# Clipping the two probability pairs of an attention step in one instruction, from a joint tile with three buffers

## The chip, the cores and the metric

The kernel runs on one core of a Trainium2 chip. The metric is the device time of one execution in microseconds (us). The engines are TensorE (PE, with its weight loads shown as PEld), VectorE (DVE), ScalarE (ACT), GpSimd (POOL) and SyncE (SP, which issues DMAs).

## The reference, cut to what matters

A cross attention with 16 heads of 32 columns, then a feed-forward part. Four batch elements, 512 query rows and 1601 context rows each. What bears on the change is the attention:

```python
scores = jnp.einsum('bhsd,bhtd->bhst', q, k) / sqrt(32)
scores = jnp.clip(scores, -50.0, 50.0)
scores = jnp.where(attend, scores, -10000.0)
scores = jnp.clip(scores, -50.0, 50.0)
probs = softmax(scores); probs = probs / (probs.sum(-1) + 1e-08)
ctx = jnp.einsum('bhst,bhtd->bhsd', probs, v)
delta = layernorm(rs * (ctx @ Wo.T + bo)) * gamma + beta
x = x + delta
x = x + ffn(layernorm(x))      # Hadamard transforms, up/gate 512 -> 2048, silu, down 2048 -> 512
```

The kernel clips after the exponential instead: between exp(-50) and exp(50), the constants `LOW` and `HIGH`.

## The kernel before, in words

The function `context` handles the four batch elements one after another. For each one there is a stretch that projects the context to keys and values, and then an attention stretch. The feed-forward part (`ffn`) follows after the fourth.

An attention stretch has four chunks c of four heads. A chunk has 13 steps t, one for each tile of 128 context rows (the last has 65). `STEPS` is 52 steps for a batch element; a step is called i, and its two pairs of heads are the pairs 2i and 2i+1, called here the first and the second pair (z = 0 and z = 1). All pairs of a program are numbered N. The work of a step is:

- PE, `scores(b, i)`, L1097: 12 matmuls into two of the three PSUM buffers `sc` (each 128 x 1024). It waits once, until the first exponential of step i-1 is done, since its second pair takes the buffer of that one.
- ACT, `exps`, L864: one exponential for each pair, 128 x 1024 f32, from `sc` into the pair's `probs` buffer.
- DVE, `clips`, L995: one clip for each pair, in place.
- DVE, `add`, L958: the sum of a pair over two adjacent steps, into `padd`. Steps 2j and 2j+1 of a chunk are added to each other. The first pair's add (z = 0) is issued in the odd step 2j+1, right behind that step's clips. The second pair's add (z = 1) is issued one step later, in the even step 2j+2, again behind the clips of that step. The 13th step has no partner.
- PE, `values`, L1110: 4 products with f32 data (8 matmuls in the trace), for which both pairs of the step have to be clipped. `sums`, L1122, and `single`, L1129, add up the rows of `padd` with a matrix of ones.

PE's order is written out by hand: scores of step i+1, then `weigh` of step i-1, which is sums and values. ACT copies the products of a chunk out in step 1 of the next chunk (`collect_values`, L842) and the sums in step 4 (`collect_sums`, L848), between the two exponentials of that step. DVE also takes a small reciprocal (`chain.recips`, L278) behind the adds of step 9 of each chunk but the first.

The buffers: the first pair has three `probs` buffers, the second pair four. Before ACT writes a pair of step i it waits, on its own queue, until the step that used this buffer last is done with it: its values product, and its add (the semaphore `added[z]`). For the first pair that is step i-3, for the second pair step i-4:

```python
old = N // 2 - BUFS[n % 2]
if old >= 0:
    act.wait_ge(values_done, old + 1)
    og, ot = divmod(old, TT)
    if ot < TT - 1:
        act.wait_ge(added[n % 2], og * QP + ot // 2 + 1)
```

Of the kernel before, what the change touches and what calls it, by code (L numbers as in the profile page):

```python
# [25 lines left out]
ALU = mybir.AluOpType  # L26
ACT = mybir.ActivationFunctionType

B, S, H, T = 4, 512, 512, 1601
# [3 lines left out]
P = 128  # L33
# [6 lines left out]
LOW = float(np.float32(np.exp(-50.0)))  # L40
HIGH = float(np.float32(np.exp(50.0)))
# [576 lines left out]
def context(nc, io, scr, proj, chain, hand):  # L618
# [1 line left out]
    STEPS = HC * TT  # L620
    PAIRS_B = 2 * STEPS
    NSC = 3
    BUFS = (3, 4)
    QP = TT // 2
    SUMS = 2 * QP + 1
    SCALE = 1.0 / float(np.sqrt(HD))
# [1 line left out]
    with ExitStack() as stack:  # L628
        m = Mem(nc, stack, "cx")
# [7 lines left out]
        q = m.at("q", [P, 2, HC, S], qslab, F32R)  # L637
        slab = m.slab("slab", Room.SIZE)
        HEADS = 2 * S * 4
        probs = [[m.at(f"probs{z}_{i}", [P, 2, S], slab + (BUFS[0] * z + i) * HEADS)[:] for i in range(BUFS[z])] for z in range(2)]  # L640
        padd = [[m.at(f"padd{z}_{i}", [P, 2, S], slab + (sum(BUFS) + 2 * z + i) * HEADS)[:] for i in range(2)] for z in range(2)]
        ob, os = (m.at(n, [P, S], slab + (sum(BUFS) + 4) * HEADS + i * S * 4)[:] for i, n in enumerate(("ob", "os")))
        sc = [m.ps(f"sc{i}", [P, 2, S]) for i in range(NSC)]
        acc, tot = m.ps("acc", [P, S]), m.ps("tot", [P, S])
        kv = [sc[0][:, 0], sc[0][:, 1], sc[1][:, 0], sc[1][:, 1]]
# [9 lines left out]
        scores_done, exp_done, clip_done, values_done, sums_done = (m.sem(n) for n in (  # L655
            "scores_done", "exp_done", "clip_done", "values_done", "sums_done"))
# [13 lines left out]

        def prob(N):

            return probs[N % 2][N // 2 % BUFS[N % 2]]

        def rows_of(t):
            return TLAST if t == TT - 1 else P

        with nc.Block() as block:
# [123 lines left out]
            def _(act):  # L802
# [47 lines left out]
                def exps(b):  # L850
                    for n in range(PAIRS_B):
                        N = b * PAIRS_B + n
                        c, t = divmod(n // 2, TT)
                        r = rows_of(t)
                        act.wait_ge(scores_done, N + 1)
# [6 lines that stand above are left out]
                            else:  # L862
                                act.wait_ge(sums_done, og * SUMS + SINGLE)
                        nc.scalar.activation(prob(N)[0:r], sc[n % NSC][0:r], ACT.Exp, bias=mbias[0:r, b, t:t + 1],  # L864
                                             scale=SCALE).then_inc(exp_done, 1)
                        if c and n % 2 == 0 and t == 1:
                            collect_values(b, c - 1)
                        if c and n % 2 == 0 and t == 4:
                            collect_sums(b, c - 1)
                    collect_values(b, HC - 1)  # L870
                    collect_sums(b, HC - 1)
# [60 lines left out]
            def _(dve):  # L932
# [15 lines left out]
                def add(b, c, j, z):  # L948
                    g = b * HC + c
                    i = b * STEPS + c * TT + 2 * j  # L950
                    dve.wait_ge(clip_done, 2 * i + 3 + z)
                    if b and c == 0 and j == 0:
                        dve.wait_ge(chain.xs_stored, b * 16)
                    if g == 0 and j == 0:
                        dve.wait_ge(ugw_out, 16)
                    if j >= 2 or g:
                        dve.wait_ge(sums_done, sums_until(g, j - 2) if j >= 2 else sums_until(g - 1, QP + j - 2))
                    nc.vector.tensor_tensor(padd[z][(g * QP + j) % 2][:], prob(2 * i + z)[:], prob(2 * i + 2 + z)[:],  # L958
                                            ALU.add).then_inc(added[z], 1)
# [29 lines left out]
                def clips(b):  # L989
                    for n in range(PAIRS_B):  # L990
                        N = b * PAIRS_B + n
                        c, t = divmod(n // 2, TT)
                        r = rows_of(t)
                        dve.wait_ge(exp_done, N + 1)
                        nc.vector.tensor_scalar(prob(N)[0:r], prob(N)[0:r], LOW, HIGH, ALU.max, ALU.min).then_inc(clip_done, 1)  # L995
                        if t % 2 and n % 2:
                            add(b, c, t // 2, 0)
                        if t and t % 2 == 0 and n % 2:
                            add(b, c, t // 2 - 1, 1)
                        if c and t == 9 and n % 2:  # L1000
                            chain.recips(nc, dve, b, c - 1)
# [19 lines left out]
                for b in range(B):  # L1021
# [44 lines left out]
                    if b + 1 < B:  # L1066
                        proj.split_lo(nc, dve, b + 1, 0)
                        proj.split_lo(nc, dve, b + 1, 1)
                    clips(b)

            @block.tensor
# [431 lines left out]
def build(nc, io, out):  # L1503
    def scratch(name, shape, dt=F32):
        return nc.dram_tensor(f"scr_{name}", shape, dt).ap()

    scr = {
        "q": scratch("q", [B, P, 2, HC, S]),
        "c": scratch("c", [B, P, HC, S]),
        "sum": scratch("sum", [B, NH, S]),  # L1510
        "rec": scratch("rec", [B, NH, S]),
        "wo": scratch("wo", [P, 2, HC, H]),
        "x1": scratch("x1", [B, P, ST, H]),
        "xs": scratch("xs", [B, 2, P, HC, S]),
        "wd": scratch("wd", [P, INTER // P, 2, H]),
        "ug": scratch("ug", [P, 2, 2, HC, GC * P]),
    }

    with ExitStack() as stack:
        m = Mem(nc, stack, "all")  # L1520
        chain = Chain(m)
        proj = Projections(Mem(nc, stack, "proj"))
        hand = Handover(Mem(nc, stack, "hand"), proj.slab)
        context(nc, io, scr, proj, chain, hand)
        ffn(nc, io, scr, out, chain, hand)
# [40 lines left out]
```

## Time and profile before

| | us |
|---|---|
| median of 3 runs | 1597.52 |
| lowest, highest | 1591.58, 1601.28 |
| the profiled execution's own time | 1598.8 |
| its span | 1597.0 |
| PE busy | 1518.2 (95%) |
| DVE busy | 984.1 (62%) |
| ACT busy | 746.0 (47%) |
| mean granted TensorE clock | 0.965 |

The span runs from the first to the last instruction, so the time holds 1.8 us around it. The busy times are shares of the whole span; the attention stretches are only four parts of it, and there the shares are others.

### The profile page before, as it was taken

How to read it: one execution, taken by the hardware profiler on the slowest of the kernel's cores; microseconds unless marked ns; L12 is line 12 of the kernel's file. 1: busy time of each engine (PE TensorE's matmuls, PEld its weight loads, DVE VectorE, ACT ScalarE, POOL GpSimd, SP SyncE). 2: the span in 40 equal slices, each digit the busy share in tenths (PEclk: the TensorE clock that was granted, in tenths of full speed). 3: DMA queues.
4: the chain of work that ended last, by engine and by line, in shares of the span. 5: the costliest groups of instructions: out<-in, count | busy, mean ns of one | idle time of the engine just before them, and what ended most of it. 6: DMA issues, size and time to landing. Idle time of an engine off the chain costs nothing. (4 is left out here: it accounts for less than half of the span.)

```text
span 1597.0 us, 25675 instructions
## 1 busy us (share of the span) xinstructions
PE 1518.2 (95%) x10712; PEld 1027.0 (64%) x10712; DVE 984.1 (62%) x1548; ACT 746.0 (47%) x923; POOL 51.1 (3%) x71
## 2 busy tenths in 40 slices
PE   5999999898899989899989999899999999999998
PEld 5887333685433578433568433376888888888886
DVE  5553999585699595699685599655434333243333
ACT  4334899233699533699633699523212212112111
POOL 1000000100000100000100000000000000000000
PEclk9998999899799999799999899999999999999999
DMA  8342000643200443100442500270201001010002
GB/s 241 138 143 119 8 9 9 178 142 104 89 9 16 134 139 110 53 9 15 126 147 84 237 9 16 54 270 11 69 0 54 27 27 53 0 53 27 0 27 79
DMA packets 56252, 121.18 MB, mean 76 GB/s; under 512 B 15680, under 2 KB 35408, under 8 KB 51536
## 3 DMA queue, kind: packets, MB, share of 16 engines
q1 hardware_dynamic: 43440, 70.04, 12.9%
q0 software_dynamic: 12704, 49.61, 9.7%
q8 instruction: 80, 1.31, 0.3%
q14 instruction: 28, 0.23, 0.1%
HBM read 82.64 MB, written 36.96 MB: 75 GB/s over the span
## 5 line engine op out<-in xcount | busy, mean ns | idle before, releaser
L864 ACT ACTIVATE cx_probs<-cx_sc,proj_mbias 128x1024 f32<-128x1024 f32 (+1 forms) x416 | 442.7, 1114 | 43.0 <-PE cx_sc L1097 35.6
L995 DVE TENSOR_SCALAR cx_probs<-cx_probs 128x1024 f32<-128x1024 f32 (+1 forms) x416 | 270.1, 684 | 33.9 <-ACT cx_probs L864 32.5
L1097 PEld LDWEIGHTS cx_sc<-cx_q,cx_kt 32*128 32x128 f32 (+1 forms) x2496 | 104.4, 185 | 203.1 <-ACT cx_probs L864 185.7
L958 DVE TENSOR_TENSOR cx_padd<-cx_probs,cx_probs 128x1024 f32<-128x1024 f32 x192 | 233.8, 1218 | 1.4 <-DVE cx_probs L995 0.7
L1110 PE MATMUL cx_acc<-cx_probs,cx_vt 128*32 128x512 f32 (+1 forms) x1664 | 222.4, 607 | 3.8 <-DVE cx_probs L995 3.8
L1097 PE MATMUL cx_sc<-cx_q,cx_kt 32*128 32x512 f32 (+1 forms) x2496 | 208.0, 435 | 17.5 <-ACT cx_probs L864 14.1
L136 PE MATMUL cx_sc<-proj_cs,proj_wk 128*128 128x256 f32 (+1 forms) x1344 | 174.5, 291 | 18.0 <-DVE proj_cs L614 13.5
L136 PEld LDWEIGHTS cx_sc<-proj_cs,proj_wk 128*128 128x128 f32 x1344 | 170.1, 199 | 22.8 <-issue 16.7
L136 PE MATMUL cx_sc<-proj_wv,proj_cs 128*128 128x512 f32 (+1 forms) x624 | 164.2, 423 | 9.6 <-DVE cx_kt L939 9.6
L136 PEld LDWEIGHTS cx_sc<-proj_wv,proj_cs 128*128 128x128 f32 (+1 forms) x624 | 123.0, 200 | 42.6 <-DVE cx_kt L939 9.7
L1122 PE MATMUL cx_tot<-cx_padd,cx_ones 128*32 128x256 f32 x1536 | 120.8, 390 | 0.0
L1416 DVE SCALAR_TENSOR_TENSOR ff_hf<-ff_up,ff_scale,ff_silu 128x512 f32<-128x512 f32 x32 | 24.0, 750 | 145.8 <-ACT ff_silu L1356 145.8
L1356 ACT ACTIVATE ff_silu<-ff_gp,ff_scale 128x512 f32<-128x512 f32 x32 | 22.1, 690 | 189.6 <-PE ff_gp L136 189.6
L1416 DVE SCALAR_TENSOR_TENSOR ff_hf<-ff_up,hand_scale,ff_silu 128x512 f32<-128x512 f32 x32 | 24.0, 750 | 129.3 <-ACT ff_silu L1356 129.2
L1356 ACT ACTIVATE ff_silu<-ff_gp,hand_scale 128x512 f32<-128x512 f32 x32 | 22.1, 690 | 165.0 <-PE ff_gp L136 165.0
L136 PE MATMUL ff_yp<-hand_wds,ff_hs 128*128 128x512 f32 x384 | 96.8, 401 | 0.0
L136 PE MATMUL ff_yp<-ff_wds,ff_hs 128*128 128x512 f32 x384 | 94.7, 395 | 0.2 <-DVE ff_hs L1419 0.2
L939 DVE SCALAR_TENSOR_TENSOR cx_kt<-cx_sc,proj_bk,cx_kt 128x256 fp32r<-128x256 f32 (+1 forms) x112 | 49.2, 450 | 67.1 <-ACT cx_kt L814 66.9
L814 ACT ACTIVATE cx_kt<-cx_sc,proj_bk 128x256 fp32r<-128x256 f32 (+1 forms) x112 | 49.2, 450 | 84.1 <-PE cx_sc L136 83.9
L136 PEld LDWEIGHTS ff_yp<-hand_wds,ff_hs 128*128 128x128 f32 x384 | 73.1, 191 | 18.1 <-issue 0.5
L136 PEld LDWEIGHTS ff_yp<-ff_wds,ff_hs 128*128 128x128 f32 x384 | 72.0, 188 | 17.7 <-DVE ff_hs L1419 0.6
L1110 PEld LDWEIGHTS cx_acc<-cx_probs,cx_vt 128*32 128x32 f32 (+1 forms) x1664 | 51.5, 111 | 49.1 <-DVE cx_probs L995 10.6
(233 smaller groups left out, 1699.0 us busy)
## 6 DMA issues: line engine op xcount, KB each, us to landing
proj_raw<-in_ctxT SPq DMA_DIRECT2D x24, 512.0 KB, 4.2
scr_q<-cx_q SPq DMA_DIRECT2D x3, 2048.0 KB, 8.2
cx_wo<-scr_wo POOLq DMA_DIRECT2D x3, 2048.0 KB, 13.1
scr_xs<-cx_xs POOLq DMA_DIRECT2D x3, 2048.0 KB, 6.8
cx_q<-scr_q SPq DMA_DIRECT2D x3, 1536.0 KB, 11.0
cx_qxt<-in_x SPq DMA_DIRECT2D x4, 1024.0 KB, 9.4
scr_c<-cx_ob SPq DMA_DIRECT2D x16, 256.0 KB
cx_fl<-in_wdT POOLq DMA_DIRECT2D x4, 1024.0 KB, 7.7
```

Source lines behind the costliest of these rows:

```text
L136: last = nc.tensor.matmul(out, stationary(a, c), moving(z, c), start=first and n == 0, stop=final and n == len(parts) - 1)
L814: nc.scalar.activation(kt[:, 0, c, t0:t0 + w], kv[c][:, 0:w], ACT.Identity, bias=bk[:, c:c + 1]).then_inc(k_hi, 1)
L864: nc.scalar.activation(prob(N)[0:r], sc[n % NSC][0:r], ACT.Exp, bias=mbias[0:r, b, t:t + 1], scale=SCALE).then_inc(exp_done, 1)
L939: nc.vector.scalar_tensor_tensor(kt[:, 1, c, t0:t0 + w], kv[c][:, 0:w], bk[:, c:c + 1], kt[:, 0, c, t0:t0 + w].bitcast(F32), ALU.add, ALU. ...
L958: nc.vector.tensor_tensor(padd[z][(g * QP + j) % 2][:], prob(2 * i + z)[:], prob(2 * i + 2 + z)[:], ALU.add).then_inc(added[z], 1)
L995: nc.vector.tensor_scalar(prob(N)[0:r], prob(N)[0:r], LOW, HIGH, ALU.max, ALU.min).then_inc(clip_done, 1)
L1097: last = nc.tensor.matmul(sc[(2 * i + h // 2) % NSC][0:r, h % 2], kt[own, z, c, t * P:t * P + r], q[own, y, c], start=n == 0, stop=n == 2)
L1110: last = nc.tensor.matmul(acc[h * HD:(h + 1) * HD], vt[0:r, t, (4 * c + h) * HD:(4 * c + h + 1) * HD], prob(N + h // 2)[0:r, h % 2], start ...
L1122: last = nc.tensor.matmul(tot[h * HD:(h + 1) * HD, cols], ones[:], padd[h // 2][(g * QP + j) % 2][:, h % 2, cols], start=j == 0 and half = ...
L1356: nc.scalar.activation(silu[u % 2][:], gp[buffer(u, first)][:], ACT.Silu, scale=scale[k][:, 1, u % GC:u % GC + 1]).then_inc(silu_done, 1)
L1416: nc.vector.scalar_tensor_tensor(hf[u % 2][:], up[buffer(u, first)][:], scale[k][:, 0, u % GC:u % GC + 1], silu[u % 2][:], ALU.mult, ALU.m ...
```

## The change

The probabilities of a step's two pairs stand side by side in one tile of 128 x 4 x 512 f32. There are three of these tiles, used in turn by the steps. The second pair thus has three buffers where it had four; `padd`, `ob` and `os` keep their addresses. DVE waits in each step until both exponentials are done and clips all four heads in one instruction of 128 x 2048 elements, which counts two on `clip_done`. The ACT waits are computed by the unchanged lines quoted above from the new `BUFS`, so that for either pair the earlier user of the buffer is now step i-3. Where the adds are issued stays as it was, and so do PE's order and all amounts of work.

```diff
-    BUFS = (3, 4)
+    BUFS, PADD = (3, 3), 7
...
-        probs = [[m.at(f"probs{z}_{i}", [P, 2, S], slab + (BUFS[0] * z + i) * HEADS)[:] for i in range(BUFS[z])] for z in range(2)]
-        padd = [[m.at(f"padd{z}_{i}", [P, 2, S], slab + (sum(BUFS) + 2 * z + i) * HEADS)[:] for i in range(2)] for z in range(2)]
+        probs = [m.at(f"probs{i}", [P, 4, S], slab + 2 * i * HEADS)[:] for i in range(BUFS[0])]
+        padd = [[m.at(f"padd{z}_{i}", [P, 2, S], slab + (PADD + 2 * z + i) * HEADS)[:] for i in range(2)] for z in range(2)]
...
         def prob(N):
-            return probs[N % 2][N // 2 % BUFS[N % 2]]
+            return probs[N // 2 % BUFS[0]][:, N % 2 * 2:N % 2 * 2 + 2]
...
-                        dve.wait_ge(exp_done, N + 1)
-                        nc.vector.tensor_scalar(prob(N)[0:r], prob(N)[0:r], LOW, HIGH, ALU.max, ALU.min).then_inc(clip_done, 1)
+                        if n % 2:
+                            both = probs[N // 2 % BUFS[0]][0:r]
+                            dve.wait_ge(exp_done, N + 1)
+                            nc.vector.tensor_scalar(both, both, LOW, HIGH, ALU.max, ALU.min).then_inc(clip_done, 2)
```

## Rows read from the trace of the kernel before

**Rows 1.** Window of the first attention stretch: length, busy PE, PEld, DVE, ACT, POOL, clock, DMA

```profile
156.90:281.00 124.10, 121.49 (x1400) 46.42 (x1404) 116.59 (x152) 112.94 (x111) 1.68 (x1) 0.96 0.03 9
```

**Rows 2.** Timelines of ACT, DVE and PE in order of time, two steps of chunk 0

```profile
180.03 2.12 ACT L864 ACTIVATE cx_probs<-cx_sc,proj_mbias 128x1024 f32<-128x1024 f32 x2 [0.21 <-PE cx_sc L1097]
182.36 2.12 ACT L864 ACTIVATE cx_probs<-cx_sc,proj_mbias 128x1024 f32<-128x1024 f32 x2 [0.20 <-PE cx_sc L1097]
...
180.73 1.22 DVE L958 TENSOR_TENSOR cx_padd<-cx_probs,cx_probs 128x1024 f32<-128x1024 f32 x1
181.87 1.29 DVE L995 TENSOR_SCALAR cx_probs<-cx_probs 128x1024 f32<-128x1024 f32 x2
183.07 1.22 DVE L958 TENSOR_TENSOR cx_padd<-cx_probs,cx_probs 128x1024 f32<-128x1024 f32 x1
...
181.35 0.97 PE L1097 MATMUL cx_sc<-cx_q,cx_kt 32*128 32x512 f32 x12
```

**Rows 3.** Waits within 170 to 280 us: who waited for whom

```profile
PEld cx_sc L1097 <- ACT cx_probs L864: 38.6, 46, 0.9
ACT cx_probs L864 <- PE cx_sc L1097: 6.3, 31, 0.2
```

**Rows 4.** Groups by line and shape, DVE

```profile
L995 DVE TENSOR_SCALAR cx_probs<-cx_probs 128x1024 f32<-128x1024 f32 x384 | 249.6, 684 | 33.9 <-ACT cx_probs L864 32.5
L958 DVE TENSOR_TENSOR cx_padd<-cx_probs,cx_probs 128x1024 f32<-128x1024 f32 x192 | 233.8, 1218 | 1.4 <-DVE cx_probs L995 0.7
...
L543 DVE TENSOR_SCALAR cx_qxt<-cx_qxt,cx_mean,cx_inv 128x512 f32<-128x512 f32 x16 | 7.7, 543 | 0.1
...
L285 DVE TENSOR_TENSOR cx_ca<-cx_ca,cx_rb 128x512 f32<-128x512 f32 x12 | 7.5, 685 | 0.0
...
L278 DVE RECIPROCAL all_recip<-all_total 128x16 f32<-128x16 f32 x16 | 3.9, 246 | 39.9 <-DMA all_total<-scr_sum 39.9
```

**Rows 5.** Timeline, ACT and DVE, first step of the first stretch

```profile
156.93 2.12 ACT L864 ACTIVATE cx_probs<-cx_sc,proj_mbias 128x1024 f32<-128x1024 f32 x2
158.07 0.70 DVE L995 TENSOR_SCALAR cx_probs<-cx_probs 128x1024 f32<-128x1024 f32 x1 [1.47 <-ACT cx_probs L864]
```

**Rows 6.** Timeline, DVE, small instructions that each wait for the last

```profile
597.30 0.16 DVE L102 TENSOR_TENSOR all_tmp<-all_inv 128x4 f32<-128x4 f32 x1
597.50 0.17 DVE L104 TENSOR_TENSOR all_tmp<-all_tmp,all_ve 128x4 f32<-128x4 f32 x1
```

**Rows 7.** Timeline, DVE and ACT, an exponential that waits for an add

```profile
474.73 1.22 DVE L958 TENSOR_TENSOR cx_padd<-cx_probs,cx_probs 128x1024 f32<-128x1024 f32 x1
...
476.06 3.31 ACT L864 ACTIVATE cx_probs<-cx_sc,proj_mbias 128x1024 f32<-128x1024 f32 x3 [0.34 <-DVE cx_padd L958]
```

**Rows 8.** Timeline, ACT: chunk 0's steps 3 and 11; chunk 2 from step 0

```profile
166.09 2.12 ACT L864 ACTIVATE cx_probs<-cx_sc,proj_mbias 128x1024 f32<-128x1024 f32 x2 [1.33 <-PE cx_sc L1097]
...
184.68 2.12 ACT L864 ACTIVATE cx_probs<-cx_sc,proj_mbias 128x1024 f32<-128x1024 f32 x2 [0.20 <-PE cx_sc L1097]
...
220.09 3.31 ACT L864 ACTIVATE cx_probs<-cx_sc,proj_mbias 128x1024 f32<-128x1024 f32 x3 [0.33 <-DVE cx_padd L958]
223.31 0.60 ACT L842 ACTIVATE cx_ob<-cx_acc 128x512 f32<-128x512 f32 x1
223.81 3.35 ACT L864 ACTIVATE cx_probs<-cx_sc,proj_mbias 128x1024 f32<-128x1024 f32 x3
...
250.75 3.31 ACT L864 ACTIVATE cx_probs<-cx_sc,proj_mbias 128x1024 f32<-128x1024 f32 x3 [0.38 <-DVE cx_padd L958]
```

**Rows 9.** Windows, PE only: length, busy, granted clock, DMA share, GB/s

```profile
180.00:280.00 100.00, 100.00 (x1192) 1.00 0.03 10
560.00:573.00 13.00, 9.64 (x30) 0.74 0.46 141
```

**Rows 10.** Timeline, PE, at the lower clock, step 3 of the first stretch

```profile
164.40 1.65 PE L1097 MATMUL cx_sc<-cx_q,cx_kt 32*128 32x512 f32 x12
165.98 1.62 PE L1110 MATMUL cx_acc<-cx_probs,cx_vt 128*32 128x512 f32 x8
```

More of the change, by code:

```diff
@@ L639, in context @@
         HEADS = 2 * S * 4
-        probs = [[m.at(f"probs{z}_{i}", [P, 2, S], slab + (BUFS[0] * z + i) * HEADS)[:] for i in range(BUFS[z])] for z in range(2)]
-        padd = [[m.at(f"padd{z}_{i}", [P, 2, S], slab + (sum(BUFS) + 2 * z + i) * HEADS)[:] for i in range(2)] for z in range(2)]
-        ob, os = (m.at(n, [P, S], slab + (sum(BUFS) + 4) * HEADS + i * S * 4)[:] for i, n in enumerate(("ob", "os")))
+        probs = [m.at(f"probs{i}", [P, 4, S], slab + 2 * i * HEADS)[:] for i in range(BUFS[0])]
+        padd = [[m.at(f"padd{z}_{i}", [P, 2, S], slab + (PADD + 2 * z + i) * HEADS)[:] for i in range(2)] for z in range(2)]
+        ob, os = (m.at(n, [P, S], slab + (PADD + 4) * HEADS + i * S * 4)[:] for i, n in enumerate(("ob", "os")))
         sc = [m.ps(f"sc{i}", [P, 2, S]) for i in range(NSC)]
```

## The prediction

> **What bounds the kernel now.** The change touches only the four attention stretches, so I read these and leave the rest. First the window of one: it is 124 us long, and in it PE is busy for 121, DVE for 117 and ACT for 113 [rows 1]; the others are alike, and the four hold 495 us of the span. Three engines are nearly full, so busy time says nothing here, and I went to the timeline. There a step takes 182.36 - 180.03 = 2.33 us on ACT. ACT's two exponentials last 2.12 together, and then it waits 0.20 for the scores [rows 2]. The list of waits has the other half of that loop: PE's loads for the scores wait for ACT 46 times, ACT for the scores 31 times [rows 3]. So the period is a ring of two engines: the first exponential, the scores that need its PSUM buffer, the next first exponential. DVE is a third thing that just fits: the add starts at 180.73 and at 183.07 again, 2.34 us per step, in which the two clips hold the engine for 183.07 - 181.87 = 1.20 and the add for 181.87 - 180.73 = 1.14 [rows 2]. DVE follows behind ACT and has no slack, and at a chunk's first step an exponential already waits 0.34 us for an add [rows 7].
>
> **What the change does to DVE's work.** It removes 208 clip instructions of 684 ns and makes the other 208 twice as large. The trace has no such instruction of 2048 elements. From above: two durations, 1.37 us. From below: an instruction of the same kind with 512 elements takes 543 ns against 684 for 1024 [rows 4], though with two pointer operands; growth of 0.14 for 512 elements would give 0.97. In between: an add takes 685 ns for 512 elements and 1218 for 1024, the clip takes for 1024 what the add takes for 512 [rows 4], so it moves two elements in the time of one and should take for 2048 what an add takes for 1024: 1.22 us. I take this one, as the rate is that of its own 1024 row. Behind an instruction that it doesn't depend on, the next one starts 0.08 before the recorded end (1.22 against 1.14 for the add), so the joint clip holds DVE for 1.14 against 1.20: a gain of 0.06 us a step. The Trainium skill (VectorE: DVE Perf Modes, section on the perf-mode tier table) gives 1227 ns for an f32 tensor_scalar of 2048 elements; the rows come to the same.
>
> **What it adds: two dependences.** The joint clip can't start before the second exponential is done. A clip that finds DVE free starts 158.07 - 156.93 = 1.14 us after the start of its exponential [rows 5]. The first pair's add (odd steps) needs that step's clip of the first pair. Before, the other clip lay between the two; now it follows the joint clip itself. Small instructions that wait for the one in front start 0.04 after its end (597.30 + 0.16 against 597.50) [rows 6], so this add starts 1.26 after the joint clip, not 1.14. The second pair's add (even steps) reads the two steps before and waits for nothing new.
>
> **What it adds: the third buffer of the second pair.** This is the term that decides. The second exponential of an odd step i now needs the buffer of step i-3, an even one. That buffer is read by the second pair's add, which is issued in the even step i-1 behind this step's clip. Before, with four buffers, it needed step i-4's, whose add is long past. So in steps 3, 5, 7, 9, 11 and in step 0 of the next chunk ACT waits for work that DVE begins only after the second exponential of the step just before: at least 1.14 (its exponential) + 1.14 (joint clip) + 1.22 (add) + an end-to-start delay of 476.06 - 475.95 = 0.11 [rows 7] = 3.61 us after that exponential's start, where one step has 2.33. It can't be hidden: ACT is in order, so queued behind the blocked exponential is the next step's first one, and behind that PE's scores and DVE's next clip.
>
> **The ring of two steps.** Start at the second exponential of an odd step (time 0). Its clip starts at 1.14. The dependent add starts at 2.40 and holds DVE until 3.54. ACT meanwhile runs the even step's exponentials at 1.01 and 2.02 (two last 2.12, the second alone 1.11 [rows 2, 7], so they start 1.01 apart), whose clip could start at 3.16, but DVE is free only at 3.54. Then the add of the second pair starts at 4.68, ends at 5.90, and the next odd step's second exponential starts at 6.01. I take 6.00 for two steps against 4.66: **+1.34**. PE needs only 2.33 a step for all its work and fits inside: its scores of the odd step follow the even step's first exponential.
>
> **The other intervals.** From step 0 to step 3 of the next chunk: ACT also copies the products in step 1, which puts the exponential behind it 0.50 later (223.81 - 223.31) [rows 8]. Step 1's clip starts at 1.01 + 0.50 + 1.01 + 1.14 = 3.66, its add at 4.92, step 2's clip at 6.06, its add at 7.20, and step 3's second exponential at 8.52. From 3 to 5, with the other copy in step 4, the clip of step 4 starts at 3.66 as well, and the interval is 6.12. From 11 over the 13th step to 0: 6.00, as it has the same clips and adds. The reciprocal (246 ns [rows 4]) behind step 9's add is on this ring too: +0.2.
>
> **The sum.** A whole chunk: 8.52 + 6.12 + 4 x 6.00 + 0.2 = 38.84, against 250.75 - 220.09 = 30.66 before [rows 8]: +8.18, three times in a stretch. Chunk 0 has the ring from step 3 to step 11 only, four intervals: 24.0 against 184.68 - 166.09 = 18.59 [rows 8]: +5.4; for the first block about +0.2. Behind step 11 of the last chunk nothing waits for an add on ACT, and its last add ends as before, 5.9 us after the second exponential of step 11. A stretch: 3 x 8.18 + 5.6 = 30.1; four: **+120 us**. On the profiled execution's 1598.8 this is 1719; on the median of 1597.52, which is 1.3 lower, it is **1718 us**. All else I cost at nothing: the loads of the next batch element run beside the attention and only gain room, POOL's preparation waits for the end of the stretch as before, and the feed-forward part is the same. If a stretch's load was hidden before, it stays so.
>
> **Bounds.** With the clip at 0.97 the ring is 1.14 + 1.01 + 1.14 + 0.89 + 1.22 + 0.11 = 5.51; the stretches have 4 x 23 = 92 blocked exponentials, and 92 x 0.49 = 45 less gives 1673. The clip at 1.37 adds 0.15 twice, 28 in all: 1746. Without the cost of the dependent add (0.12 each): 1707.
>
> **Rivals.**
> 1. **The ring is on ACT, not on DVE.** DVE isn't recharged by the odd step, so that the even step's clip starts at 3.16: 3.16 + 1.14 + 1.22 + 0.11 = 5.63 for two steps, 0.37 less in some 92 intervals: 1684. For it speaks that the margin is only 3.54 - 3.16; against it, that both of its numbers come from rows. Chance 0.08.
> 2. **Faster: the block doesn't bind and DVE's queue gets shorter.** The place is the second exponential of odd steps; if the add were done before ACT comes there, only the 0.06 us a step would be left, on the engine that has no slack: 208 x 0.06 = 12, 1585. The Trainium skill (VectorE: DVE Perf Modes, rules for kernel authors) says to minimise the number of operations, which read alone gives this result. It decides once ACT comes to the exponential 3.61 us after that of the step before; the trace has 2.33 [rows 2], 1.28 short. Chance 0.03.
> 3. **TensorE's clock falls.** PE would be busy for 4.66 of 6.00, 78%. Where it was busy for 9.64 of 13 us, the mean granted clock was 0.74; in the full stretch it was 1.00 [rows 9]. The lower one of the two levels (1.2 GHz) makes scores last 1.65 and values 1.62 [rows 10] against 0.97 in scores [rows 2]; a step's PE work grows to about 4, and two steps to 8: up to 104 x 2 = 208 more, 1926. Against it: at that level PE would be busy without a gap, and after such a stretch the clock rose again (from 167 us on). Chance 0.05.
> 4. **The joint clip runs at the add's rate**, one element at a time: about 2.28 instead of 1.22, 2 x 1.07 more in an interval, 92 x 2.14 = 197: 1915. The instruction differs from the present one only in its length. Chance 0.03.
>
> **How the numbers follow.** The forecast with its own spread (1700 to 1740) has 0.76, rival 1 has 0.08, a clip much cheaper than taken 0.02, the dearer ones 0.03 between 1740 and 1750, the others as above. The range 1680 to 1745 leaves out rivals 2 to 4 and the cheap clip. What a measurement here can tell from no change is about 1%. Faster by over 1%: 0.02; within 1%: 0.02; slower: 0.96.
>
> **What the changed kernel's profile would show.** Attention windows of 154 us instead of 124, with DVE and ACT busy shares near 0.76 and 0.73. One group of clips of 128 x 2048, 208 of them, at 1.22. On ACT's timeline, at 6.0 us a repeat: the second exponential of an odd step and both of the even step in one run; then the odd step's first one, which itself needs the first pair's add of two steps back (at 2.40 + 1.22 + 0.11 = 3.73); then, some 1.2 us idle after its end, the blocked one. So ACT waits for `padd` L958 over 92 times, where such waits were few and short (0.34). Nothing before 157 us changed, and the feed-forward part as long as before. The prediction is wrong if ACT finds the add done, if two steps take well under 5.6 us, or if the clock row of the attention windows falls below 0.9.

## The result and the profile after

The changed kernel takes 1734.1 us (median of 4 runs, 1730.3 to 1737.8), the kernel before 1597.4 in the same comparison: a ratio of 1.0859, 95% interval 1.0817 to 1.0900. That is 137 us more, where 120 were forecast. The profiled execution took 1735.2 us with a span of 1733.3, against 1598.8 and 1597.0.

First the windows of the four attention stretches in the changed kernel, all engines (length, then busy time and instructions of PE, PEld, DVE, ACT and POOL, then granted clock, DMA share and GB/s); the first one answers to [rows 1].

```profile
157.00:312.70 155.70, 125.00 (x1404) 46.43 (x1404) 116.11 (x101) 112.87 (x111) 1.18 (x1) 0.97 0.03 8
446.90:602.50 155.60, 124.91 (x1400) 46.48 (x1404) 116.04 (x101) 112.87 (x110) 1.19 (x1) 0.97 0.03 8
724.30:879.30 155.00, 124.25 (x1404) 46.13 (x1404) 116.09 (x101) 112.84 (x111) 1.21 (x1) 0.98 0.03 8
999.80:1154.70 154.90, 123.19 (x1404) 45.78 (x1404) 116.06 (x101) 112.78 (x111) 0.00 (x0) 0.99 0.13 53
```

They hold 621.2 us where they held 495.1: +126.1. The engines have the same work as before (DVE 116.1 us a stretch, ACT 112.9), only spread over 155 us, so no instruction became dearer; there are waits. The remaining 10 us of the span lie outside these windows.

The same two steps on the timelines of ACT and DVE, which answer to [rows 2]:

```profile
185.72 3.13 ACT L864 ACTIVATE cx_probs<-cx_sc,proj_mbias 128x1024 f32<-128x1024 f32 x3 [1.15 <-PE cx_sc L1099]
189.54 1.12 ACT L864 ACTIVATE cx_probs<-cx_sc,proj_mbias 128x1024 f32<-128x1024 f32 x1 [0.69 <-DVE cx_padd L958]
191.81 3.11 ACT L864 ACTIVATE cx_probs<-cx_sc,proj_mbias 128x1024 f32<-128x1024 f32 x3 [1.15 <-DVE cx_padd L958]
```

```profile
184.38 1.22 DVE L958 TENSOR_TENSOR cx_padd<-cx_probs,cx_probs 128x1024 f32<-128x1024 f32 x1
186.93 1.23 DVE L997 TENSOR_SCALAR cx_probs<-cx_probs 128x2048 f32<-128x2048 f32 x1 [1.33 <-ACT cx_probs L864]
188.20 1.23 DVE L958 TENSOR_TENSOR cx_padd<-cx_probs,cx_probs 128x1024 f32<-128x1024 f32 x1
189.34 1.22 DVE L997 TENSOR_SCALAR cx_probs<-cx_probs 128x2048 f32<-128x2048 f32 x1
190.47 1.22 DVE L958 TENSOR_TENSOR cx_padd<-cx_probs,cx_probs 128x1024 f32<-128x1024 f32 x1
193.03 1.23 DVE L997 TENSOR_SCALAR cx_probs<-cx_probs 128x2048 f32<-128x2048 f32 x1 [1.33 <-ACT cx_probs L864]
```

The reader should walk the ring through both fences. The run of three exponentials that begins at 185.72 is the blocked one of an odd step and both of the even step. The joint clip follows at 186.93, the dependent add at 188.20, the next joint clip at 189.34, the second pair's add at 190.47. That ends at 191.69, and the next blocked exponential starts at 191.81, 6.09 us after the first. Where both idle times of 1.15 end 0.12 behind the end of an add (184.38 + 1.22 = 185.60 for the first), the profile puts one down to PE and the other to DVE: a releaser is inferred, and the ends in the timeline decide.

Two groups and one wait of the changed kernel, to be read beside [rows 3, 4]:

```profile
L997 DVE TENSOR_SCALAR cx_probs<-cx_probs 128x2048 f32<-128x2048 f32 x192 | 234.7, 1222 | 159.3 <-ACT cx_probs L864 159.2
L958 DVE TENSOR_TENSOR cx_padd<-cx_probs,cx_probs 128x1024 f32<-128x1024 f32 x192 | 234.5, 1221 | 3.3
```

```profile
ACT cx_probs L864 <- DVE cx_padd L958: 94.2, 120, 1.3
```

The joint clip takes 1.222 us. DVE, which had no slack, now idles 159 us before these clips, and ACT waits 120 times for adds.

### The profile page after: what moved, and what is told of

The parts are those of the page before. It is cut to its first block and busy times, and to the rows that moved or that the text cites. A ratio compares the mean times of both kernels' runs of the same rounds, so it can differ in the third digit from the quotient of the medians.

```text
span 1733.3 us, 25676 instructions
## 1 busy us (share of the span) xinstructions
PE 1535.4 (89%) x10712; PEld 1028.5 (59%) x10712; DVE 984.5 (57%) x1340; ACT 745.1 (43%) x923; POOL 49.8 (3%) x71
## 5 line engine op out<-in xcount | busy, mean ns | idle before, releaser
L997 DVE TENSOR_SCALAR cx_probs<-cx_probs 128x2048 f32<-128x2048 f32 (+1 forms) x208 | 254.1, 1222 | 159.3 <-ACT cx_probs L864 159.2
L136 PE MATMUL cx_sc<-proj_wv,proj_cs 128*128 128x512 f32 (+1 forms) x624 | 160.5, 416 | 10.7 <-DVE cx_kt L939 10.7
```

Of the source, the lines that this page charges most:

```text
L136: last = nc.tensor.matmul(out, stationary(a, c), moving(z, c), start=first and n == 0, stop=final and n == len(parts) - 1)
L997: nc.vector.tensor_scalar(both, both, LOW, HIGH, ALU.max, ALU.min).then_inc(clip_done, 2)
```

## The experiments

**Is it the third buffer, and how much of it?** The kernel before with three buffers for the second pair, and the changed kernel with four joint tiles.

```diff
 # e1, against the kernel before
-    BUFS = (3, 4)
+    BUFS, PADD = (3, 3), 7
 # e2, against the changed kernel
-    BUFS, PADD = (3, 3), 7
+    BUFS, PADD = (4, 4), 8
-        ob, os = (m.at(n, [P, S], slab + (PADD + 4) * HEADS + i * S * 4)[:] ...
+        ob = os = m.sb("ob", [P, S])[:]
...
-        self.bo, self.gamma, self.beta = (m.sb(n, [P, H]) for n in ("bo", "gamma", "beta"))
+        self.bo, self.gamma = (m.sb(n, [P, H]) for n in ("bo", "gamma"))
+        self.beta = self.gamma
```

To have room for the fourth tile e2 differs in more: it leaves out beta (gamma stands in its place, and one constant fewer is loaded), `ob` and `os` share a buffer, and of ACT's waits for stores one asks for more and one is new.

> The kernel before with one number changed: the second pair has three buffers, clips stay two instructions. Theory (the third buffer decides): the second exponential of an odd step waits for the add issued behind the even step's clips. The ring of two steps: second clip 1.14 after its exponential, first pair's add at 1.74, DVE free at 2.88, two clips until 4.08, add 1.22, 0.11 to the exponential: 5.41 us against 4.66, 92 times 0.75 = +69 us: 1667 us. Half of the loss of the changed kernel, the other half coming only together with the joint clip. Rival (the joint clip and its wait for both exponentials are the cause alone): 1597 us, two steps stay at 4.66.

Measured: 1669.8 us (1667.3 to 1672.8), ratio 1.0446, interval 1.0417 to 1.0476: +73 us. The timelines of ACT and DVE in e1:

```profile
208.75 2.29 ACT L864 ACTIVATE cx_probs<-cx_sc,proj_mbias 128x1024 f32<-128x1024 f32 x2
212.17 4.29 ACT L864 ACTIVATE cx_probs<-cx_sc,proj_mbias 128x1024 f32<-128x1024 f32 x4 [1.13 <-DVE cx_padd L958]
```

```profile
210.84 1.22 DVE L958 TENSOR_TENSOR cx_padd<-cx_probs,cx_probs 128x1024 f32<-128x1024 f32 x1
211.97 0.69 DVE L995 TENSOR_SCALAR cx_probs<-cx_probs 128x1024 f32<-128x1024 f32 x1
213.32 0.69 DVE L995 TENSOR_SCALAR cx_probs<-cx_probs 128x1024 f32<-128x1024 f32 x1 [0.66 <-ACT cx_probs L864]
213.93 1.22 DVE L958 TENSOR_TENSOR cx_padd<-cx_probs,cx_probs 128x1024 f32<-128x1024 f32 x1
215.06 1.29 DVE L995 TENSOR_SCALAR cx_probs<-cx_probs 128x1024 f32<-128x1024 f32 x2
216.27 1.22 DVE L958 TENSOR_TENSOR cx_padd<-cx_probs,cx_probs 128x1024 f32<-128x1024 f32 x1
```

The same picture with the old clips: from one second pair's add (210.84) to the next (216.27) it is 5.43 us, where 5.41 were expected and 4.66 is the undisturbed value. In this form only the second clip (213.32) has to wait behind the blocked exponential; the first one is already done. So the missing buffer alone makes half of the loss.

> The changed kernel with four joint tiles in place of three. For room, beta's buffer is given up (gamma's stands in for it, so the output lacks beta), and ob and os share one buffer. Theory: with four tiles no exponential waits for an add of the step before; what is left of the change is DVE's queue: 1.14 + 1.14 a step, 0.12 more where the add depends on the clip: 4.68 us for two steps against 4.66, so 1597 to 1610 us. Rival (the late joint clip hurts by itself, by the dependent add or late values): more than half of the loss stays, over 1665 us.

Measured: 1601.7 us (1596.5 to 1606.2), ratio 1.0024, interval 1.0005 to 1.0043. With four tiles 132 of the 137 us are gone. DVE in e2:

```profile
208.38 1.22 DVE L961 TENSOR_TENSOR cx_padd<-cx_probs,cx_probs 128x1024 f32<-128x1024 f32 x1
209.51 1.22 DVE L1000 TENSOR_SCALAR cx_probs<-cx_probs 128x2048 f32<-128x2048 f32 x1
210.77 1.23 DVE L961 TENSOR_TENSOR cx_padd<-cx_probs,cx_probs 128x1024 f32<-128x1024 f32 x1
211.91 1.22 DVE L1000 TENSOR_SCALAR cx_probs<-cx_probs 128x2048 f32<-128x2048 f32 x1
213.04 1.22 DVE L961 TENSOR_TENSOR cx_padd<-cx_probs,cx_probs 128x1024 f32<-128x1024 f32 x1
```

Two steps take 213.04 - 208.38 = 4.66 us again, with the joint clip. One add starts 1.26 behind its clip (the dependent one, 209.51 to 210.77), the other 1.13 (211.91 to 213.04). The rival, that the joint clip hurts by itself, falls: without the buffer wait it costs nothing in the ring, and without the joint clip the buffer wait costs 73. The other half of the loss is the two together. What e2 still loses lies behind the stretches: these take 487.9 us in its profile (488.6 and 490.6 in two profiles of the kernel before), but at each stretch's end the last values product comes 5.4 us after the second exponential of the last chunk's step 11, where it came after 4.9.

**Is it the buffer, or how late its add stands?** The changed kernel with the second pair's add in the odd step (e3), and the same move on top of e1 (e5).

```diff
                         if t % 2 and n % 2:
                             add(b, c, t // 2, 0)
-                        if t and t % 2 == 0 and n % 2:
-                            add(b, c, t // 2 - 1, 1)
+                            add(b, c, t // 2, 1)
```

> The changed kernel with the second pair's add issued in the odd step, behind the first pair's, no longer behind the even step's clip. Theory: the wait for the buffer stays, but what it waits for is earlier: 1.22 after the odd exponential the clip, 1.26 more the first add, 1.14 more the second, 1.34 to the exponential two steps on: 4.96 us for two steps against 6.09, so 1630 us or a little under. Rival (the joint clip's own cost): no change from 1734 us.

Measured: 1632.6 us (1627.8 to 1641.7), ratio 1.0224, interval 1.0174 to 1.0273. ACT in e3:

```profile
208.25 4.29 ACT L864 ACTIVATE cx_probs<-cx_sc,proj_mbias 128x1024 f32<-128x1024 f32 x4 [0.66 <-DVE cx_padd L958]
213.22 4.29 ACT L864 ACTIVATE cx_probs<-cx_sc,proj_mbias 128x1024 f32<-128x1024 f32 x4 [0.67 <-DVE cx_padd L958]
```

4.97 us for two steps against the 4.96 worked out. Moving one add in the queue, with the buffers and the joint clip unchanged, gives back 101 us.

> As e1 (two clips, three buffers for either pair), and both adds of two steps are issued in the odd step, behind its clips. Theory (it is not the number of buffers but the distance from the add to the exponential that needs it): the second pair's add ends 1.14 + 0.60 + 1.14 + 1.22 = 4.10 us after the odd step's second exponential starts, 4.21 with the 0.11 behind it, and that exponential comes 4.66 later, so nobody waits: 1597 to 1603 us with one buffer fewer than the kernel before. Rival (three buffers are too few wherever the add stands): 1620 us or more, as in e1 or e3.

Measured: 1604.1 us (1599.7 to 1613.7), ratio 1.0042, interval 1.0020 to 1.0064. The ring is free: e5's exponentials run from 156.2 to 1024.2 us, and two steps take 4.67. With the adds in the right place three buffers are enough. But 6 us are left that the ring doesn't hold (the stretches take 488.5 us); e7 below takes them up.

**Is one long instruction dearer than two?**

```diff
-                            nc.vector.tensor_scalar(both, both, LOW, HIGH, ALU.max, ALU.min).then_inc(clip_done, 2)
+                            for z in range(2):
+                                nc.vector.tensor_scalar(both[:, 2 * z:2 * z + 2], both[:, 2 * z:2 * z + 2], LOW, HIGH, ALU.max, ALU.min).then_inc(clip_done, 1)
```

> The changed kernel with the joint clip issued as two instructions of 1024 elements, both behind the wait for the second exponential. Theory (it is the waiting, not the length of the instruction): the add no longer depends on the instruction in front of it (0.12 less), the two clips hold DVE 1.20 and not 1.14 (0.06 more, twice): 6.10 us for two steps against 6.09, 1734 us, within 5. Rival (a single long instruction is dearer than two): at least 10 us faster.

Measured: 1724.9 us (1719.9 to 1732.2), ratio 1.0812, interval 1.0773 to 1.0851: 9 us less than the changed kernel, which is between the theory's 5 and the rival's 10 and so meets neither, and the intervals of both kernels overlap. The timeline tells how much is the ring's. ACT and DVE in e4:

```profile
217.39 3.13 ACT L864 ACTIVATE cx_probs<-cx_sc,proj_mbias 128x1024 f32<-128x1024 f32 x3 [1.23 <-DVE cx_padd L958]
223.42 2.12 ACT L864 ACTIVATE cx_probs<-cx_sc,proj_mbias 128x1024 f32<-128x1024 f32 x2 [1.23 <-DVE cx_padd L958]
```

```profile
218.53 1.30 DVE L998 TENSOR_SCALAR cx_probs<-cx_probs 128x1024 f32<-128x1024 f32 x2 [1.26 <-ACT cx_probs L864]
```

6.03 us for two steps, not 6.09. The small clip starts 1.14 after its exponential did (217.39 to 218.53), the joint one 1.21 (185.72 to 186.93 above). So waiting ahead of both clips costs what the joint clip costs, and one long instruction saves nothing: it starts 0.07 later than a short one. The ring's part is small: e4's stretches take 613.0 us against 616.7. What the other few microseconds are isn't settled by this run.

**Would DVE's shorter queue pay once nothing waits?** e2 with both adds ahead of the even step's clip:

```diff
-                        if t % 2 and n % 2:
-                            add(b, c, t // 2, 0)
+                        if t and t % 2 == 0 and n % 2:
+                            add(b, c, t // 2 - 1, 0)
+                            add(b, c, t // 2 - 1, 1)
                         if n % 2:
                             both = probs[N // 2 % BUFS[0]][0:r]
...
-                        if t and t % 2 == 0 and n % 2:
-                            add(b, c, t // 2 - 1, 1)
```

> As e2 (joint clip, four tiles, gamma in beta's place, one buffer for ob and os), and both adds of two steps are issued in the next even step ahead of its clip, so that no add depends on the instruction in front. DVE then holds 4 x 1.14 = 4.56 us in two steps, not 4.68. Theory (the ring of exponential and scores sets 2.33 a step whatever DVE does): 1597 to 1602 us, no gain over e2 beyond 5 us. Rival (DVE's queue is what sets the period, so that the joint clip can pay once its waits are gone): 104 x 0.10 = 10 us less, 1587 to 1591 us.

Measured: 1612.7 us (1606.7 to 1615.5), ratio 1.0093, interval 1.0068 to 1.0117: 11 us slower than e2. Both numbers expected were missed, the rival's sign too. In mid-chunk two steps still take 4.67 us on ACT, so DVE's queue isn't what sets the period: the ring of exponential and scores does. A new loss is at chunk ends. With two adds ahead of it, the 13th step's clip is late for the values product. PE and ACT in e6:

```profile
192.89 1.06 PE L1114 MATMUL cx_acc<-cx_probs,cx_vt 65*32 65x512 f32 x8 [0.36 <-DVE cx_probs L1003]
...
194.02 0.60 ACT L843 ACTIVATE cx_ob<-cx_acc 128x512 f32<-128x512 f32 x1 [0.35 <-PE cx_acc L1114]
```

ACT copies that product out between two exponentials and stands 0.35 us for it. The four stretches take 492.9 us in this profile, 5.0 more than in e2's. The other 6 of the 11 us it can't show: its execution, 1606.7 us, was the fastest of e6's six.

**Where do the 10 us outside the attention stretches come from?** Both kernels were profiled once more.

> The kernel before, profiled once more. The changed kernel's profile is 126 us longer in the attention stretches and 10 us longer in the rest. Theory: the rest varies from run to run with where TensorE's lower clock falls, so that this profile's rest differs from 1106 us by several us. Rival: it is 1106 again and the 10 us belong to the change.

> The changed kernel, profiled once more. Theory: the rest outside the attention stretches differs from 1117 us by several us, the attention stretches are 617 us again. Rival: both are the same again.

Measured: spans of 1593.8 and 1740.1 us. From the first to the last exponential's start, the stretches of the changed kernel sum to 616.8 us (616.7 in its first profile), those of the kernel before to 488.6 (490.6). The rest is 1123.3 and 1116.7 with the change, 1105.2 and 1106.4 without. The pairs don't overlap, and they are 14 us apart. But both profiled executions of the changed kernel, 1735.2 and 1742.0 us, lie above its median of 1734.1; by the medians the rest is about 10 us longer. Single profiles scatter by as much as that: e4, with nearly the same stretches as the changed kernel and gaps of 1.00 and 1.27 us on PE at their ends, has a rest of 1105.0, in the fastest of its four executions. The two profiles of the kernel before differ by 1.2 us in the rest, as the rival had it, those of the changed kernel by 6.6, as the theory had it. So some 10 us belong to the change, and two profiles don't fix the number. The timeline of PE at the end of the first stretch, in the second profile of the kernel before, and then in the changed kernel:

```profile
281.06 1.04 PE L1110 MATMUL cx_acc<-cx_probs,cx_vt 128*32 128x512 f32 x8
283.03 1.07 PE L1110 MATMUL cx_acc<-cx_probs,cx_vt 65*32 65x512 f32 x8 [0.93 <-DVE cx_probs L995]
286.18 1.09 PE L136 MATMUL cx_sc<-proj_cs,proj_wk 128*128 128x256 f32 x7
```

```profile
312.04 1.06 PE L1112 MATMUL cx_acc<-cx_probs,cx_vt 128*32 128x512 f32 x8 [0.93 <-DVE cx_probs L997]
314.43 1.06 PE L1112 MATMUL cx_acc<-cx_probs,cx_vt 65*32 65x512 f32 x8 [1.33 <-DVE cx_probs L997]
```

PE's one gap has become two, of 0.93 and 1.33. Yet the gaps by themselves make nothing later: the last values product starts 4.89 us after the second exponential of the last chunk's step 11 (309.54 to 314.43), in the kernel before 4.86 (278.17 to 283.03). What differs is how long the work right behind them takes. PE at the end of the second stretch, in the first profile of the kernel before, and then in the changed kernel:

```profile
538.63 1.06 PE L1110 MATMUL cx_acc<-cx_probs,cx_vt 65*32 65x512 f32 x8 [1.04 <-DVE cx_probs L995]
541.79 2.41 PE L136 MATMUL cx_sc<-proj_cs,proj_wk 128*128 128x256 f32 x18
```

```profile
604.45 1.94 PE L1112 MATMUL cx_acc<-cx_probs,cx_vt 65*32 65x512 f32 x8 [1.33 <-DVE cx_probs L997]
610.58 1.65 PE L136 MATMUL cx_sc<-proj_cs,proj_wk 128*128 128x256 f32 x11
```

The last values product takes 1.94 us instead of 1.06, and the first projection product follows 6.13 us after it instead of 3.16. In the two profiles of the kernel before this distance is 3.15 or 3.16 us behind each of the first three stretches, and 6.18 behind the fourth, where PE idles another 3 us. In the changed kernel it is 3.15, 6.13, 3.15 and 8.80 us in the first profile, 4.43, 6.13, 6.13 and 9.12 in the second: together 5.6 and 10.2 us more. The granted clock shows the same. Windows of PE alone that begin with the last exponential of the second and of the fourth stretch (length, busy time, granted clock, DMA share, GB/s), for the kernel before and then for the changed one:

```profile
535.90:555.90 20.00, 18.95 (x156) 1.00 0.82 245
...
1018.50:1058.50 40.00, 33.21 (x169) 0.91 0.59 187
```

```profile
601.40:621.40 20.00, 18.02 (x118) 0.83 0.65 178
...
1153.60:1193.60 40.00, 32.33 (x140) 0.79 0.51 167
```

In the same time PE does 118 matmuls and not 156, and 140, not 169. In the two profiles of the kernel before all six windows behind the first three stretches have the full clock; of the changed kernel's six, four have 0.83 to 0.91. The kernel before isn't free of the lower clock: in the next 20 us it has 0.74 to 0.91 six times too, and the changed kernel 0.83 to 0.91. Two runs tested this end of a stretch by itself: e7 is e5 with the very last add of a stretch back behind the last clips, e8 the changed kernel with the last two steps clipped pair by pair.

```diff
 # e7, against e5
-                            add(b, c, t // 2, 1)
+                            if (c, t) != (HC - 1, TT - 2):
+                                add(b, c, t // 2, 1)
+                        if (c, t) == (HC - 1, TT - 1) and n % 2:
+                            add(b, c, t // 2 - 1, 1)
 # e8, against the changed kernel
-                        if n % 2:
+                        if c == HC - 1 and t >= TT - 2:
+                            dve.wait_ge(exp_done, N + 1)
+                            nc.vector.tensor_scalar(prob(N)[0:r], prob(N)[0:r], LOW, HIGH, ALU.max, ALU.min).then_inc(clip_done, 1)
+                        elif n % 2:
```

> As e5, but the last add of the second pair in a stretch stands again behind the last step's clips, as in the kernel before. In e5 the attention stretches are as fast as before (488.5 us), yet PE has a gap of 1.85 us behind each stretch's last scores where the kernel before has 0.93, and TensorE's lower clock falls more often into what follows. Theory (the end of the stretch and the clock behind it make up e5's 6 us): 1597 to 1600 us. Rival (they are scatter, or belong to the three buffers): 1603 to 1605 us as e5.

Measured: 1597.5 us (1589.8 to 1604.6), ratio 0.9998, interval 0.9980 to 1.0015, as expected. The gap is 0.70 where e5 had 1.84:

```profile
283.05 1.06 PE L1112 MATMUL cx_acc<-cx_probs,cx_vt 65*32 65x512 f32 x8 [0.70 <-DVE cx_probs L995]
```

PE has 4.6 us less gap at the four ends together, and the time is 6.6 us less than e5's; with the two intervals this can be the gaps alone. The profiles have a hint of more: from the last values product to the first projection product e5 takes 4.07, 3.15 and 4.84 us behind the first three stretches, e7 3.15 each time.

> The changed kernel, but in the last two steps of each stretch the pairs are clipped one by one as in the kernel before. The ring stays at 6.09 us. Theory (a part of the loss outside the attention stretches is the late joint clip at their end, which leaves PE gaps, and the lower clock behind them): 0.1 to 0.4 us less gap four times and fewer low stretches, 1726 to 1731 us. Rival (no part of it): 1734 us.

Measured: 1723.1 us (1714.0 to 1730.8), ratio 1.0777, interval 1.0750 to 1.0804: 11 us less than the changed kernel and more than expected, with the attention stretches unchanged (616.4 us). The first gap is 0.33 here, the second 1.27, and the last values product comes some 0.65 us sooner behind the second exponential of step 11 (4.23 at three ends, 4.45 at one), which is 2.6 us at four ends. So by the times the late joint clip at the ends has a part in the loss outside the stretches. How the other 8 us come about isn't shown: e8's profile, of the slowest of its six executions, still has a clock of 0.83 behind two of the first three stretches. Nor does it take a joint clip: e1 has none, has a gap of 1.27 at the ends, and 0.83 behind two of the first three as well. That the lower clock is the link between a gap of a microsecond and these losses is read from the timelines and windows; no run changed the clock by itself.

**A version that beats both?** The end of a stretch was the one place with slack to win, so e9 is the kernel before with the first pair's last add moved behind the last clips:

```diff
-                        if t % 2 and n % 2:
+                        if t % 2 and n % 2 and (c, t) != (HC - 1, TT - 2):
                             add(b, c, t // 2, 0)
+                        if (c, t) == (HC - 1, TT - 1) and n % 2:
+                            add(b, c, t // 2 - 1, 0)
```

> The kernel before with one move: in the last chunk of a stretch the first pair's last add stands behind the last step's clips, no longer in front of them. These clips come 1.14 us earlier, and PE's gap of 0.93 us behind the stretch should close. Theory: 4 x 0.9 = 3.6 us less and perhaps as much again by the clock: 1590 to 1594 us. Rival (PE then waits for the sums instead): 1597 us.

Measured: 1595.4 us (1589.0 to 1600.9), ratio 0.9989, interval 0.9971 to 1.0007. The gap fell from 0.93 to 0.44 us, half of what was hoped, and the time doesn't differ measurably. No version here beats the kernel before.

## Why the prediction was right, and where it was off

- **The third buffer, "the term that decides".** Right, and shown from both sides: four joint tiles give back all but 5 us (e2), the missing buffer alone costs 73 (e1), an earlier add gives back 101 with three buffers (e3).
- **The ring of two steps, 6.00 us.** It is 6.09. All its terms were within 0.01 us of the rows (clip to dependent add 1.27, add to clip 1.14, clip to add 1.13, add to exponential 1.34) but one: the joint clip starts 1.21 after its exponential and not 1.14, since that value came from a clip of half the length (e4's short clips have 1.14 again). 92 x 0.07 = 6 us, the whole of 126 against the predicted 120.
- **The clip at 1.22 us.** 1.222. The two bounds, 0.97 and 1.37, weren't needed.
- **"All else I cost at nothing".** This is the step that failed. Within the stretch the end is as forecast: the last add ends 5.97 us after the second exponential of step 11, where 5.9 were taken, and the last values product starts within 0.03 us of where it did (0.14 behind the second stretch). But PE comes to that end with gaps of 0.93 and 1.33 us in place of 0.93, and the work right behind them, more often at the lower clock, took 5.6 and 10.2 us more in the two profiles. By the medians the loss outside the stretches is 10 us, and the sum had nothing for it. e8 takes 11 off by earlier clips at the ends; how the gaps, the ring's waits and the clock share the loss stays open.
- **The number.** 1718 was forecast and 1734.1 measured. Of the 16 us between them 6 are the clip's later start and 10 are this.
- **Rival 1 (the ring is on ACT).** Wrong: the even step's joint clip starts at 189.34, where the odd step's add lets DVE go, and not on its own exponential.
- **Rival 2 (faster).** Wrong in two ways. The block binds; and where it doesn't (e2, e6), DVE's shorter queue gives nothing, since ACT and PE set 4.66 for two steps. Fewer instructions have no time to give here.
- **Rival 3 (the clock falls).** Not inside the stretches: 0.97 to 0.99 there, with PE busy for about 80%. A small part of it did happen, at the places behind the stretches, where neither the rival nor the sum looked.
- **Rival 4 (one element at a time).** Wrong, by the 1.222 us.

## What to carry to other kernels

Before a buffer is taken from a rotation, look for who frees it last, and in which position of its engine's queue that instruction stands: a use that is issued one round late turns "three buffers" into two. Joining instructions of two producers makes the first one's result as late as the second's; add up that ring from rows before counting what the shorter queue saves. And look at the ends of a pipelined stretch separately, as the steady state tells nothing about who waits there.

## What was not expected of the hardware

A clip on DVE that waits for ACT starts later when it is longer: 1.22 us after the start of its exponential with 2048 elements (changed kernel), 1.15 with 1024 (e4), each the median of 116 such waits in the same place of the loop. And short idle times of PE went with a lower clock right behind them. Gaps of 0.93 and 1.33 us at the end of a stretch in which PE was busy for about 80% were followed by a granted clock of 0.83 to 0.91 in four of six windows of 20 us; one gap of 0.92 to 1.05 us at the end of a stretch in which it was busy for 98% had 1.00 behind it in all six. Whether the gaps or the partly idle stretch matters, no run here separates.
